# Spline weight stages: small tables spread inside SBUF instead of full-height tables, and DMAs moved between three queues

## The chip, the cores and the metric

The kernel runs on the 8 cores of one Trainium2 chip, each core with its own quarter-batch half and no exchange between cores. The time is the device time of the slowest core, in microseconds.

## The reference

One transformer layer in "sandwich" form over x of shape (4, 2048, 2048): attention (16 heads, causal), then a gated feed-forward network whose three weight matrices are not given but are interpolated from control points.

```python
def spline_reconstruct(control_points, out_size, in_size):
    n = out_size * in_size
    idx, f = _catmull_rom_grid(control_points.shape[0], n)   # n_ctrl = n / 128.9
    p0, p1, p2, p3 = (control_points[idx[k]] for k in range(4))
    w = 0.5*(2*p1 + (p2-p0)*f + (2*p0-5*p1+4*p2-p3)*f**2 + (3*p1-p0-3*p2+p3)*f**3)
    return w.reshape(out_size, in_size)

gate_w, up_w = spline_reconstruct(gate_cp, 8192, 2048), spline_reconstruct(up_cp, 8192, 2048)
down_w = spline_reconstruct(down_cp, 2048, 8192)

x = x + layernorm(attention(layernorm(x)))
h = layernorm(x)
x = x + layernorm((silu(h @ gate_w.T) * (h @ up_w.T)) @ down_w.T)
```

## The kernel before

Each core builds all three weight matrices for itself and holds them in DRAM (`wbuf_g`, `wbuf_u`, `wbuf_d`). 128 consecutive weights form a block that spans at most two spline segments, so a block's weights are a product of 16 numbers (4 control points times 4 powers of a position) with a fixed 16x128 matrix (`atsb`), once for each of the two segments; a byte mask says for each weight which of the two holds. There are NBLK = 131072 blocks.

**Gate/up stage** (`make_gu_gen`, the first stage, 64 chunks of GCH = 2048 blocks). Per chunk:

1. `ldtoks(c)` loads two fp32 tables of 128 rows, `cpr0` (control points) and `tpr0` (powers), on GpSimd's queue, cast to bf16 in flight, into `gi0`, `gi1` (2 buffers each). Many of the 128 rows are repeats: only 10 rows of control points and 8 of powers are distinct.
2. `umult(c)` (VectorE, L363) multiplies them into `Ug`.
3. For the gate tile (w = 0), then for the up tile (w = 1), four groups of 512 blocks: two matmuls (L396) into `pguA`, `pguB`; ScalarE copies `pguB` to `gwo` (L412); VectorE overwrites it from `pguA` where the mask `gm` is set (L417). These last are called evictions here.
4. After four groups SyncE's queue stores the tile: `wbuf_g`, then `wbuf_u`, 512 KB each. `gwo` has two buffers, one for each w, so ScalarE's first copy of a tile waits for that tile's store in the chunk before. Behind the up store SyncE's queue loads the mask for chunk c+2.

The loads for c+1 are written ahead of the matmuls of c and wait for `umult(c-1)`.

**Down stage** (`make_down_gen`, 32 chunks of DCH = 4096 blocks, after attention and the output projection). The same with one tile of eight groups a chunk, tables of 64 rows (`cpr1`, `tpr1`), and lines L465 (multiply), L495 (matmuls), L509 (copy), L513 (eviction). Its store is 1 MB in runs of 64 bf16 numbers (128 B), 8192 of them, into `wbuf_d`; `dwo` has two buffers, by c % 2. Store and mask load (`dm`, 512 KB) share SyncE's queue.

Engines run their instructions in program order. A DMA stands in the order of its issuing engine, and whatever it waits for holds what is behind it. `Sched` writes the order out by hand: letters T, V, S, G, Y are TensorE, VectorE, ScalarE, GpSimd, SyncE. All DMA issues show line L160.

The stages between and after (`x2T` norm and transpose, QKV projection `pq` L629, attention, output projection `po` L843, feed-forward `pgE` L1021, `puE` L1027, `pdE` L1070) are separated from these two by barriers on all engines.

Of the kernel before, what the change touches and what calls it, by code (L numbers as in the profile page):

```python
# [10 lines left out]
F32 = mybir.dt.float32  # L11
BF16 = mybir.dt.bfloat16
# [3 lines left out]
AP = bass.AP  # L16

B, S, D = 4, 2048, 2048
# [4 lines left out]
NBLK = NSAMP // 128  # L23
GCH = 2048
NGCH = NBLK // GCH
DCH = 4096
NDCH = NBLK // DCH
# [252 lines left out]
def build_program():  # L280
    nc = bass.Bass("TRN2", target_bir_lowering=False)
    sch = Sched()
# [5 lines left out]
    bout_d = nc.dram_tensor("bout_rep", [128, D], F32, kind="ExternalInput")  # L288
    cpr0 = nc.dram_tensor("cpr0", [128, NBLK], F32, kind="ExternalInput")
    cpr1 = nc.dram_tensor("cpr1", [64, NBLK], F32, kind="ExternalInput")  # L290
    tpr0 = nc.dram_tensor("tpr0", [128, NBLK], F32, kind="ExternalInput")
    tpr1 = nc.dram_tensor("tpr1", [64, NBLK], F32, kind="ExternalInput")
# [17 lines left out]
    with ctx:  # L310
# [20 lines left out]

        def make_gu_gen(wc, pA, pB, depth):
            U = [wc.enter_context(nc.sbuf_tensor(f"Ug{i}", [128, GCH], BF16))
                 for i in range(2)]
# [5 lines left out]
                nc.sbuf_tensor(f"gm_{i}", [128, GCH], mybir.dt.uint8))  # L340
                for i in range(2)]
            WO = [wc.enter_context(nc.sbuf_tensor(f"gwo_{i}", [128, GCH], BF16))
                  for i in range(2)]
            streams = [(wbuf_g, 0, 32), (wbuf_u, 64, 96)]

            def ldtoks(c):
                t0 = sch.dma("G", IN0[c % 2][:, :],
                             AP(cpr0, c * GCH, [[NBLK, 128], [1, GCH]]),
                             f"wg{c % 2}")
                t1 = sch.dma("G", IN1[c % 2][:, :],  # L350
                             AP(tpr0, c * GCH, [[NBLK, 128], [1, GCH]]),
                             f"wg{c % 2}")
                return (t0, t1)

            def gen():
                umark, evmark, stok, mtoks, ltok = {}, {}, {}, {}, {}

                def umult(c):
                    sch.wait("V", ltok[c][0])
                    sch.wait("V", ltok[c][1])  # L360
                    if c >= 2:
                        sch.wait("V", evmark[(c - 2) * 8 + 7])
                    sch.op("V", lambda v, b=c % 2: v.tensor_mul(  # L363
                        U[b][:, :], IN0[b][:, :], IN1[b][:, :]))
                    umark[c] = sch.mark("V")

                for c in range(NGCH):
                    yield
                    buf = c % 2
                    if c == 0:  # L370
                        for cpre in (0, 1):
                            mtoks[cpre] = sch.dma(
                                "Y", MSK[cpre % 2][:, :],
                                wgm_gu_d[:, cpre * GCH:(cpre + 1) * GCH],
                                f"gm{cpre % 2}")
                        ltok[0] = ldtoks(0)
                        umult(0)
                    if c + 1 < NGCH:
                        if c >= 1:
                            sch.wait("G", umark[c - 1])  # L380
                        ltok[c + 1] = ldtoks(c + 1)
                    sch.wait("T", umark[c])
                    for w in range(2):
# [3 lines left out]
                        for q4 in range(4):  # L387
# [21 lines left out]
                            wo_ap = WO[cw % 2][:, q4 * 512:(q4 + 1) * 512]  # L409
                            mk_ap = MSK[c % 2][:, q4 * 512:(q4 + 1) * 512]  # L410
                            sch.op("S", lambda s, o_=wo_ap, pp=pB[bk]:
# [6 lines left out]
                            evmark[i2] = sch.mark("V")  # L418
                        sch.wait("Y", evmark[c * 8 + w * 4 + 3])
                        stok[cw] = sch.dma(  # L420
                            "Y", wb[:, c * GCH:(c + 1) * GCH],
                            WO[cw % 2][:, :],
                            f"ws{cw % 2}")
                    if c + 2 < NGCH:
                        sch.wait("Y", evmark[c * 8 + 7])
                        mtoks[c + 2] = sch.dma(
                            "Y", MSK[c % 2][:, :],
                            wgm_gu_d[:, (c + 2) * GCH:(c + 3) * GCH],
                            f"gm{c % 2}")
                    if c + 1 < NGCH:  # L430
# [4 lines left out]

        def make_down_gen(wc, pA, pB, depth):
            Ud = [wc.enter_context(nc.sbuf_tensor(f"Ud{i}", [64, DCH], BF16))
                  for i in range(2)]
# [5 lines left out]
                nc.sbuf_tensor(f"dm_{i}", [128, DCH], mybir.dt.uint8))  # L444
                for i in range(2)]
            WO = [wc.enter_context(nc.sbuf_tensor(f"dwo_{i}", [128, DCH], BF16))
                  for i in range(2)]
            NCG = DCH // 512

            def ldtoks(c):  # L450
                sch.dma("G", IN0[c % 2][:, :],
                        AP(cpr1, c * DCH, [[NBLK, 64], [1, DCH]]),
                        f"wd{c % 2}")
                return sch.dma("G", IN1[c % 2][:, :],
                               AP(tpr1, c * DCH, [[NBLK, 64], [1, DCH]]),
                               f"wd{c % 2}")

            def gen():
                umark, evmark, stok, mtoks, ltok = {}, {}, {}, {}, {}

                def umult(c):
                    sch.wait("V", ltok[c])
                    if c >= 2:
                        sch.wait("V", evmark[(c - 2) * NCG + NCG - 1])
                    sch.op("V", lambda v, b=c % 2: v.tensor_mul(  # L465
                        Ud[b][:, :], IN0[b][:, :], IN1[b][:, :]))
                    umark[c] = sch.mark("V")

                for c in range(NDCH):
                    yield  # L470
                    buf = c % 2
                    if c == 0:
                        for cpre in (0, 1):
                            mtoks[cpre] = sch.dma(
                                "Y", MSK[cpre % 2][:, :],
                                wgm_dn_d[:, cpre * DCH:(cpre + 1) * DCH],
                                f"dm{cpre % 2}")
                        ltok[0] = ldtoks(0)
                        umult(0)
                    if c + 1 < NDCH:  # L480
                        if c >= 1:
                            sch.wait("G", umark[c - 1])
                        ltok[c + 1] = ldtoks(c + 1)
                    sch.wait("T", umark[c])
                    first_ev = True
                    for cg in range(NCG):
# [14 lines left out]
                        if first_ev:  # L501
                            if c >= 2:
# [3 lines left out]
                        wo_ap = WO[buf][:, cg * 512:(cg + 1) * 512]  # L506
                        mk_ap = MSK[c % 2][:, cg * 512:(cg + 1) * 512]
                        sch.op("S", lambda s, o_=wo_ap, pp=pB[bk]:
# [14 lines left out]
                    if c + 2 < NDCH:  # L523
                        mtoks[c + 2] = sch.dma(
                            "Y", MSK[c % 2][:, :],
                            wgm_dn_d[:, (c + 2) * DCH:(c + 3) * DCH],
                            f"dm{c % 2}")
                    if c + 1 < NDCH:
# [616 lines left out]
def _perm_gu():  # L1145
    if "gu" not in _TPR:
        p = np.arange(GCH).reshape(GCH // 16, 16).T.ravel()
        _TPR["gu"] = (np.arange(NBLK).reshape(-1, GCH)[:, p]).ravel()
    return _TPR["gu"]


def _perm_dn():
    if "dn" not in _TPR:
        p = np.arange(DCH).reshape(DCH // 64, 64).T.ravel()
        _TPR["dn"] = (np.arange(NBLK).reshape(-1, DCH)[:, p]).ravel()
    return _TPR["dn"]


def _tpr0():
    if 0 not in _TPR:  # L1160
        cst = _consts()
        _TPR[0] = np.ascontiguousarray(
            cst["taupow"][cst["r0_tau"]][:, _perm_gu()])
    return _TPR[0]


def _tpr1():
    if 1 not in _TPR:
        cst = _consts()
        _TPR[1] = np.ascontiguousarray(  # L1170
            cst["taupow"][cst["r1_tau"]][:, _perm_dn()])
    return _TPR[1]
# [57 lines left out]
```

How the kernel before makes its waits and increments, by code:

```python
            def f(eng):  # L196
                for fn, waits, incs, _isdma in self.recs[e]:
                    agg = {}
                    for (sn, v) in waits:
                        agg[sn] = max(agg.get(sn, 0), v)
                    for sn, v in agg.items():
                        eng.wait_ge(sems[sn], v)
                    inst = fn(eng)
                    for (sn, n, _tgt) in incs:
                        inst.then_inc(sems[sn], n)
```

## Time and profile before

| | us |
|---|---|
| median of 2 runs | 4481.23 (4478.77 to 4483.7) |
| the profiled execution | 4469.14 |
| its span, slowest core (core 4) | 4467.6 |
| spans of the other cores | 4446.7 to 4462.4 |
| granted TensorE clock, mean | 0.869 to 0.871 |

The profile is of one execution on its slowest core. Busy time counts instructions of an engine; DMA share is the mean busy share of 16 DMA engines. SPq, ACTq and POOLq are the queues in which SyncE, ScalarE and GpSimd issue DMAs.

### The profile page before, as it was taken

Reading aid. Unit: us, or ns where it says so; the run is one execution under the profiler, and the core shown is the slowest. Engines: PE = TensorE matmul, PEld = TensorE weight load, DVE = VectorE, ACT = ScalarE, POOL = GpSimd, SP = SyncE. Lnnn points to the kernel's source line nnn. Section 1 sums busy time; section 2 is a strip of 40 time slices with the busy share of each in tenths; the row PEclk is TensorE's granted clock in tenths of the full one; section 3 lists DMA queues with packets and bytes.
Section 4 is the critical chain, followed back from the end, with each engine's and each line's share of the span. In section 5 each row is a group of like instructions: output and inputs, shape, how many; then the busy total and the mean of one; then the engine's idle time right before and its main releaser. Section 6 shows DMA issues by size and latency. Waiting matters only on the chain.

```text
span 4467.6 us, 40618 instructions; the slowest of 8 cores (4446.7 to 4467.6 us)
## 1 busy us (share of the span) xinstructions
PE 2937.2 (66%) x12618; PEld 1171.4 (26%) x12832; DVE 1419.7 (32%) x1868; ACT 924.6 (21%) x1519; POOL 139.9 (3%) x232
## 2 busy tenths in 40 slices
PE   2333333299999567676922222289998947999895
PEld 0000111244444111111410000044443323444332
DVE  4555565722222343433064544411000032001002
ACT  3344443200000334333112322200000021000001
POOL 1000000000000000000000000000000000000000
PEclk9999999999999777777955555589999978999997
DMA  9999997364443100000549999944433444444344
GB/s 173 191 206 206 211 211 193 122 79 74 76 76 67 58 19 29 29 29 11 84 157 162 160 157 158 147 151 152 155 145 111 138 149 158 151 151 152 108 137 141
DMA packets 588577, 567.97 MB, mean 127 GB/s; under 512 B 280016, under 2 KB 495056, under 8 KB 576976
## 3 DMA queue, kind: packets, MB, share of 16 engines
q1 hardware_dynamic: 498640, 431.11, 35.9%
q0 software_dynamic: 89728, 134.25, 20.4%
q8 instruction: 110, 1.80, 0.2%
q14 instruction: 99, 0.81, 0.1%
HBM read 565.31 MB, written 134.22 MB: 157 GB/s over the span
## 4 chain that ended last, share of the span: by engine, by line
PE 49%; DMA 25%; DVE 15%; SPq 4%; issue 4%; ACT 3%; DVEq 0%; ACTq 0%; another core or an unknown queue 0%; POOL 0%; POOLq 0%
PE pq L629 12%; DMA wbuf_g<-gwo 10%; PE puE L1027 10%; PE pgE L1021 10%; PE pdE L1070 6%; DMA wdsb<-wbuf_d 5%; DMA dm<-wgmask_dn 5%; SPq L160 4%; DVE gwo L417 4%; PE prow L222 3%; PE pav L226 3%; PE psc L764 3%; PE po L843 2%; DVE rs L799 2%; DVE colsb L236 2%
## 5 line engine op out<-in xcount | busy, mean ns | idle before, releaser
L1027 PE MATMUL puE<-x2f,wusb 128*128 128x512 bf16 x2048 | 778.4, 380 | 22.7 <-DMA wusb<-wbuf_u 18.5
L1021 PE MATMUL pgE<-x2f,wgsb 128*128 128x512 bf16 x1966 | 747.0, 380 | 0.0
L396 PE MATMUL pguA<-Ug,atsb 16*128 16x512 bf16 x512 | 267.4, 597 | 479.7 <-DVE Ug L363 266.3
L629 PE MATMUL pq<-x2T,wq 128*128 128x512 bf16 x2508 | 551.6, 380 | 17.8 <-DMA wq<-wqkvT 15.1
L1070 PE MATMUL pdE<-actsb,wdsb 128*128 128x512 bf16 x2006 | 458.4, 382 | 54.1 <-DMA wdsb<-wbuf_d 51.0
L417 DVE CAST_PREDICATED gwo<-gm,pguA 128x512 bf16<-128x512 uint8 x512 | 353.7, 691 | 301.6 <-ACT gwo L412 254.8
L495 PE MATMUL pdnA<-Ud,atsb 16*128 16x512 bf16 x256 | 133.7, 597 | 407.9 <-DVE dwo L513 214.4
L412 ACT CAST gwo<-pguB 128x512 bf16<-128x512 f32 x512 | 299.6, 585 | 435.5 <-DMA wbuf_g<-gwo 378.5
L1042 DVE TENSOR_TENSOR actsb<-silsb,puE 128x512 bf16<-128x512 bf16 x128 | 88.1, 688 | 819.0 <-ACT silsb L1037 819.0
L629 PEld LDWEIGHTS pq<-x2T,wq 128*128 128x128 bf16 x2560 | 250.9, 98 | 318.3 <-issue 17.6
L775 ACT ACTIVATE pT<-psc 128x512 bf16<-128x512 f32 x384 | 229.3, 597 | 330.5 <-PE psc L764 289.8
L1070 PEld LDWEIGHTS pdE<-actsb,wdsb 128*128 128x128 bf16 x2048 | 195.2, 98 | 317.3 <-issue 103.8
L396 PE MATMUL pguB<-Ug,atsb 16*128 16x512 bf16 x512 | 274.8, 613 | 0.0
L1021 PEld LDWEIGHTS pgE<-x2f,wgsb 128*128 128x128 bf16 x2048 | 200.9, 98 | 261.0 <-issue 20.8
L1027 PEld LDWEIGHTS puE<-x2f,wusb 128*128 128x128 bf16 x2048 | 200.8, 98 | 242.7 <-issue 2.4
L513 DVE CAST_PREDICATED dwo<-dm,pdnA 128x512 bf16<-128x512 uint8 x256 | 176.9, 691 | 258.8 <-DMA dm<-wgmask_dn 214.4
L1037 ACT ACTIVATE silsb<-pgE 128x512 bf16<-128x512 f32 x128 | 76.4, 597 | 792.3 <-PE puE L1027 792.2
L396 PEld LDWEIGHTS pguA<-Ug,atsb 16*128 16x128 bf16 x512 | 56.5, 110 | 683.8 <-issue 683.7
L509 ACT CAST dwo<-pdnB 128x512 bf16<-128x512 f32 x256 | 149.8, 585 | 384.2 <-DMA wbuf_d<-dwo 189.1
L764 PE MATMUL psc<-qall,kb 128*128 128x512 bf16 x375 | 172.1, 473 | 76.7 <-DVE attnout L713 54.5
L649 DVE TENSOR_SCALAR kst<-pq,bqkvsb 128x512 bf16<-128x512 f32 x128 | 96.1, 751 | 346.0 <-PE pq L629 346.0
L782 DVE TENSOR_TENSOR pT<-pT,cmasksb 128x512 bf16<-128x512 bf16 x256 | 109.0, 426 | 299.7 <-ACT pT L775 298.0
(76 smaller groups left out, 1960.5 us busy)
## 6 DMA issues: line engine op xcount, KB each, us to landing
wgsb<-wbuf_g SPq DMA_DIRECT2D x128, 512.0 KB, 3.7
wusb<-wbuf_u SPq DMA_DIRECT2D x128, 512.0 KB, 4.6
wdsb<-wbuf_d SPq DMA_DIRECT2D x128, 512.0 KB, 3.7
gi<-cpr POOLq DMA_DIRECT2D x64, 512.0 KB, 9.4
gi<-tpr POOLq DMA_DIRECT2D x64, 512.0 KB, 12.4
wbuf_g<-gwo SPq DMA_DIRECT2D x64, 512.0 KB, 7.3
wbuf_u<-gwo SPq DMA_DIRECT2D x64, 512.0 KB, 5.1
wbuf_d<-dwo SPq DMA_DIRECT2D x32, 1024.0 KB, 18.5
```

The costliest lines, as they stand in the source:

```text
L160: [lambda eng, o=out, i=in_: eng.dma_start(out=o, in_=i), w, [(sname, 16, tgt)], True])
L396: t.matmul(pp[:, :], at_sb[u_:u_ + 16, :], U[b][u_:u_ + 16, cc:cc + 512], start=True, stop=True, tile_position=(u_, 0)))
L412: s.copy(o_, pp[:, :]))
L417: v.copy_predicated(o_, m_, pp[:, :]))
L509: s.copy(o_, pp[:, :]))
L513: v.copy_predicated(o_, m_, pp[:, :]))
L629: t.matmul(pq[bi][:, :], wq[(o // 2) % 2][:, h * 256 + (o % 2) * 128: h * 256 + (o % 2) * 128 + 128], x2T[:, h * S + g * 512:h * S + g * 5 ...
L764: t.matmul(psc[c % 4][:, :], kb[b][:, c * 128:c * 128 + 128], q_all[:, hh * TPC + ts * 512: hh * TPC + ts * 512 + 512], start=True, stop=T ...
L775: s.activation(pT[b][:, c * 512:c * 512 + 512], psc[c % 4][:, :], AF.Exp, bias=0.0, scale=SCALE))
L1021: t.matmul(pg[bi][:, :], wg[o % 4][:, h * 128:h * 128 + 128], x2f[:, h * 512:h * 512 + 512], start=(h == 0), stop=(h == 15)))
L1027: t.matmul(pu[bi][:, :], wu[o % 4][:, h * 128:h * 128 + 128], x2f[:, h * 512:h * 512 + 512], start=(h == 0), stop=(h == 15)))
L1070: t.matmul(pd[bi + o][:, :], wd[(i_ // 8) % 2][:, (i_ % 8) * 256 + o * 128: (i_ % 8) * 256 + o * 128 + 128], act[:, i_ * 512:i_ * 512 + 51 ...
```

## The change

The change touches only the two weight stages.

- The tables are loaded small: for gate/up 10 rows of control points (`tap_gu`) and 32 of powers (`tau_gu`: 8 distinct rows, repeated to 32) into a new tile `gct`; for down 5 and 32 rows into `dct`. Still on GpSimd's queue, still cast.
- A new function `expand(c)` copies them inside SBUF into the 128-row (64-row) tiles by DMAs on ScalarE's queue, eight of 16 rows x 4 KB a chunk in gate/up, four of 16 rows x 8 KB in down. Rows that hold nothing are zeroed once by VectorE. `expand(c+1)` stands in ScalarE's program order after the gate tile of chunk c (gate/up) or after the fifth of eight groups (down), and waits for the loads of c+1.
- `umult(c)` waits for the spreads. The loads for c+1 wait for the spreads of c-1 and not for `umult(c-1)`.
- Mask loads move from SyncE's to ScalarE's queue, three chunks ahead instead of two, with four buffers instead of two.
- Stores alternate: gate tiles and even down chunks on SyncE's queue, up tiles and odd down chunks on GpSimd's.

The diff, cut to its core (down follows gate/up; its differing lines are shown):

```diff
@@ make_gu_gen
             def ldtoks(c):
-                t0 = sch.dma("G", IN0[c % 2][:, :],
-                             AP(cpr0, c * GCH, [[NBLK, 128], [1, GCH]]),
-                             f"wg{c % 2}")
-                t1 = sch.dma("G", IN1[c % 2][:, :],
-                             AP(tpr0, c * GCH, [[NBLK, 128], [1, GCH]]),
-                             f"wg{c % 2}")
-                return (t0, t1)
+                sch.dma("G", CT[c % 2][0:10, :],
+                        AP(tap_gu_d, c * GCH, [[NBLK, 10], [1, GCH]]),
+                        f"wg{c % 2}")
+                return sch.dma("G", CT[c % 2][10:42, :],
+                               AP(tau_gu_d, c * GCH, [[NBLK, 32], [1, GCH]]),
+                               f"wg{c % 2}")
...
+                def expand(c):
+                    sch.wait("S", ltok[c])
+                    if c >= 2:
+                        sch.wait("S", umark[c - 2])
+                    else:
+                        sch.wait("S", msmk_gu)
+                    for si in range(4):
+                        wt, dlt = si // 2, si % 2
+                        sch.dma("S", AP(IN0[c % 2], (si * 32) * GCH,
+                                        [[GCH, 16], [1, GCH]]),
+                                AP(CT[c % 2], (wt * 5 + dlt) * GCH,
+                                   [[GCH, 4], [0, 4], [1, GCH]]),
+                                f"we{c % 2}")
+                        etok[c] = sch.dma(
+                            "S", AP(IN1[c % 2], (si * 32) * GCH,
+                                    [[GCH, 16], [1, GCH]]),
+                            AP(CT[c % 2], (10 + dlt * 16) * GCH,
+                               [[GCH, 16], [1, GCH]]),
+                            f"we{c % 2}")
...
                 def umult(c):
-                    sch.wait("V", ltok[c][0])
-                    sch.wait("V", ltok[c][1])
+                    sch.wait("V", etok[c])
...
                     if c + 1 < NGCH:
                         if c >= 1:
-                            sch.wait("G", umark[c - 1])
+                            sch.wait("G", etok[c - 1])
                         ltok[c + 1] = ldtoks(c + 1)
...
-                        sch.wait("Y", evmark[c * 8 + w * 4 + 3])
+                        stq = "Y" if cw % 2 == 0 else "G"
+                        sch.wait(stq, evmark[c * 8 + w * 4 + 3])
                         stok[cw] = sch.dma(
-                            "Y", wb[:, c * GCH:(c + 1) * GCH],
+                            stq, wb[:, c * GCH:(c + 1) * GCH],
                             WO[cw % 2][:, :],
                             f"ws{cw % 2}")
-                    if c + 2 < NGCH:
-                        sch.wait("Y", evmark[c * 8 + 7])
-                        mtoks[c + 2] = sch.dma(
-                            "Y", MSK[c % 2][:, :],
+                        if w == 0 and c + 1 < NGCH:
+                            expand(c + 1)
+                    if c + 3 < NGCH:
+                        if c >= 1:
+                            sch.wait("S", evmark[(c - 1) * 8 + 7])
+                        mtoks[c + 3] = sch.dma(
+                            "S", MSK[(c + 3) % 4][:, :],
...
@@ make_down_gen
+                    for si in range(2):
+                        sch.dma("S", AP(IN0[c % 2], (si * 32) * DCH,
+                                        [[DCH, 16], [1, DCH]]),
+                                AP(CT[c % 2], si * DCH,
+                                   [[DCH, 4], [0, 4], [1, DCH]]),
+                                f"de{c % 2}")
...
+                        if cg == NCG // 2 and c + 1 < NDCH:
+                            expand(c + 1)
                     od = DCH // 64
-                    sch.wait("Y", evmark[c * NCG + NCG - 1])
+                    stq = "Y" if c % 2 == 0 else "G"
+                    sch.wait(stq, evmark[c * NCG + NCG - 1])
                     stok[c] = sch.dma(
-                        "Y",
+                        stq,
                         AP(wbuf_d, c * od,
                            [[64 * D, 128], [D, 64], [1, od]]),
                         AP(WO[buf], 0, [[DCH, 128], [od, 64], [1, od]]),
...
```

## Rows read from the trace of the kernel before

**Rows 1.** The page: span, and the chain that ended last by line.

```profile
span 4467.6 us, 40618 instructions; the slowest of 8 cores (4446.7 to 4467.6 us)
...
PE pq L629 12%; DMA wbuf_g<-gwo 10%; PE puE L1027 10%; PE pgE L1021 10%; PE pdE L1070 6%; DMA wdsb<-wbuf_d 5%; DMA dm<-wgmask_dn 5%; SPq L160 4%; DVE gwo L417 4%; PE prow L222 3%; PE pav L226 3%; PE psc L764 3%; PE po L843 2%; DVE rs L799 2%; DVE colsb L236 2%
```

**Rows 2.** Busy us by stage, engine by engine; then clock, DMA share, GB/s.

```profile
13.00:762.00 749.00, 276.70 (x1024) 72.16 (x1024) 432.19 (x576) 300.86 (x513) 65.44 (x124) 1.00 0.95 201
...
2341.00:2880.00 539.00, 138.38 (x512) 36.02 (x512) 249.94 (x288) 149.78 (x256) 33.19 (x64) 0.50 1.21 156
```

**Rows 3.** Timeline of gate/up chunks: start, us, engine, line, instruction, idle before.

```profile
423.99 0.32 SPq L160 DMA_DIRECT2D wbuf_u<-gwo  x1
424.02 1.23 DVE L363 TENSOR_TENSOR Ug<-gi 128x2048 bf16<-128x2048 bf16 x1
...
425.40 0.60 PE L396 MATMUL pguB<-Ug,atsb 16*128 16x512 bf16 x1
...
427.89 4.62 ACT L412 CAST gwo<-pguB 128x512 bf16<-128x512 f32 x7 [5.66 <-DMA wbuf_g<-gwo]
...
431.79 0.32 SPq L160 DMA_DIRECT2D wbuf_g<-gwo  x1
```

**Rows 4.** Gate stores by tensor: issue ns, first and last start.

```profile
L160 SPq DMA_DIRECT2D wbuf_g<-gwo x64: 319/320/326, 26.0 to 755.7; - x64
```

**Rows 5.** DMA queues in 100 us of the gate/up stage: packets, MB, share.

```profile
DMA packets 6448, 21.16 MB, mean 212 GB/s; under 512 B 714, under 2 KB 714, under 8 KB 6442
...
q0 software_dynamic: 2554, 9.31, 57.5%
q1 hardware_dynamic: 3888, 11.80, 37.9%
```

**Rows 6.** Down stores by tensor: issue ns, first and last start.

```profile
L160 SPq DMA_DIRECT2D wbuf_d<-dwo x32: 524/525/2850, 2365.3 to 2866.8; - x32
```

**Rows 7.** SyncE's queue in the down stage, first chunks.

```profile
2365.32 0.61 SPq L160 DMA_DIRECT2D wbuf_d<-dwo  x1
2365.98 7.83 SPq L160 DMA_DIRECT2D dm<-wgmask_dn  x1
```

**Rows 8.** Timeline of down chunks, later: SyncE's queue and VectorE.

```profile
2592.96 2.28 DVE L465 TENSOR_TENSOR Ud<-di 64x4096 bf16<-64x4096 bf16 x1
2593.49 15.42 SPq L160 DMA_DIRECT2D dm<-wgmask_dn  x1
...
2596.95 6.25 DVE L513 CAST_PREDICATED dwo<-dm,pdnA 128x512 bf16<-128x512 uint8 x8 [1.71 <-ACT dwo L509]
```

**Rows 9.** DMA queues in 440 us of the down stage.

```profile
q1 hardware_dynamic: 222455, 41.58, 83.1%
```

**Rows 10.** Chain in order of time: the last down store.

```profile
2866.82 12.84 DMA wbuf_d<-dwo
```

**Rows 11.** GpSimd's DMA issues by tile: count | busy, mean ns.

```profile
L160 POOL DMA_DIRECT2D gi<-cpr x64 | 33.9, 530 | 656.4 <-DVE Ug L363 653.8 <-POOLq L177 2.6
L160 POOL DMA_DIRECT2D wq<-wqkvT x24 | 27.4, 1143 | 641.8 <-PE pq L629 486.8 <-DVE x2T L583 155.0
```

**Rows 12.** DMA queues in 110 us of the QKV projection.

```profile
q0 software_dynamic: 15342, 7.79, 54.5%
```

**Rows 13.** DMA queues in 200 us of the down projection.

```profile
q1 hardware_dynamic: 53766, 27.11, 46.1%
```

**Rows 14.** GB/s in 40 slices of 23 us, K and V loads alone.

```profile
GB/s 0 12 130 313 233 235 317 354 383 385 385 351 356 392 385 413 413 399 427 385 427 363 178 57 0 0 0 0 0 0 0 0 0 0 0 0 0 0 0 0
```

**Rows 15.** A SyncE issue behind two others: ns.

```profile
L160 SPq DMA_DIRECT2D bqkvsb<-bqkv x1: 432/432/432, 2.0 to 2.0; - x1
```

**Rows 16.** DMA issues, whole run: count, KB each, median us to landing.

```profile
wgsb<-wbuf_g SPq DMA_DIRECT2D x128, 512.0 KB, 3.7
...
kvbuf<-kst SPq DMA_DIRECT2D x128, 128.0 KB, 1.8
...
atsb<-atilde POOLq DMA_DIRECT2D x4, 4.0 KB, 2.3
```

More of the change, by code:

```diff
@@ L332, in make_gu_gen @@
         def make_gu_gen(wc, pA, pB, depth):
+            CT = [wc.enter_context(nc.sbuf_tensor(f"gct{i}", [42, GCH], BF16))
+                  for i in range(2)]
             U = [wc.enter_context(nc.sbuf_tensor(f"Ug{i}", [128, GCH], BF16))
@@ L340, in make_gu_gen @@
                 nc.sbuf_tensor(f"gm_{i}", [128, GCH], mybir.dt.uint8))
-                for i in range(2)]
+                for i in range(4)]
             WO = [wc.enter_context(nc.sbuf_tensor(f"gwo_{i}", [128, GCH], BF16))
@@ L436, in make_down_gen @@
         def make_down_gen(wc, pA, pB, depth):
+            CT = [wc.enter_context(nc.sbuf_tensor(f"dct{i}", [37, DCH], BF16))
+                  for i in range(2)]
             Ud = [wc.enter_context(nc.sbuf_tensor(f"Ud{i}", [64, DCH], BF16))
@@ L444, in make_down_gen @@
                 nc.sbuf_tensor(f"dm_{i}", [128, DCH], mybir.dt.uint8))
-                for i in range(2)]
+                for i in range(4)]
             WO = [wc.enter_context(nc.sbuf_tensor(f"dwo_{i}", [128, DCH], BF16))
@@ L448, in make_down_gen, with expand @@
             NCG = DCH // 512
+            for t in IN0 + IN1:
+                sch.op("V", lambda v, t_=t: v.memset(t_[:, :], 0.0))
+            msmk_dn = sch.mark("V")
             def ldtoks(c):
-                sch.dma("G", IN0[c % 2][:, :],
-                        AP(cpr1, c * DCH, [[NBLK, 64], [1, DCH]]),
+                sch.dma("G", CT[c % 2][0:5, :],
+                        AP(tap_dn_d, c * DCH, [[NBLK, 5], [1, DCH]]),
                         f"wd{c % 2}")
-                return sch.dma("G", IN1[c % 2][:, :],
-                               AP(tpr1, c * DCH, [[NBLK, 64], [1, DCH]]),
+                return sch.dma("G", CT[c % 2][5:37, :],
+                               AP(tau_dn_d, c * DCH, [[NBLK, 32], [1, DCH]]),
                                f"wd{c % 2}")
             def gen():
-                umark, evmark, stok, mtoks, ltok = {}, {}, {}, {}, {}
+                umark, evmark, stok, mtoks = {}, {}, {}, {}
+                ltok, etok = {}, {}
+                def expand(c):
+                    sch.wait("S", ltok[c])
+                    if c >= 2:
+                        sch.wait("S", umark[c - 2])
+                    else:
+                        sch.wait("S", msmk_dn)
+                    for si in range(2):
[4 more added lines that the diff above has]
+                                f"de{c % 2}")
+                        etok[c] = sch.dma(
+                            "S", AP(IN1[c % 2], (si * 32) * DCH,
+                                    [[DCH, 16], [1, DCH]]),
+                            AP(CT[c % 2], (5 + si * 16) * DCH,
+                               [[DCH, 16], [1, DCH]]),
+                            f"de{c % 2}")
                 def umult(c):
-                    sch.wait("V", ltok[c])
+                    sch.wait("V", etok[c])
                     if c >= 2:
@@ L481, in gen @@
                         if c >= 1:
-                            sch.wait("G", umark[c - 1])
+                            sch.wait("G", etok[c - 1])
                         ltok[c + 1] = ldtoks(c + 1)
@@ L522, in gen @@
                         f"dws{c % 2}")
[L523 to L527, printed above, removed]
+                    if c + 3 < NDCH:
+                        if c >= 1:
+                            sch.wait("S", evmark[(c - 1) * NCG + NCG - 1])
+                        mtoks[c + 3] = sch.dma(
+                            "S", MSK[(c + 3) % 4][:, :],
+                            wgm_dn_d[:, (c + 3) * DCH:(c + 4) * DCH],
+                            f"dm{(c + 3) % 4}")
                     if c + 1 < NDCH:
@@ L1156, in _perm_dn, with _tau_tiled @@
     return _TPR["dn"]
+def _tau_tiled():
+    cst = _consts()
+    tp = cst["taupow"]
+    return np.concatenate([np.tile(tp[0:4], (4, 1)), np.tile(tp[4:8], (4, 1))])
 def _tpr0():
     if 0 not in _TPR:
-        cst = _consts()
-        _TPR[0] = np.ascontiguousarray(
-            cst["taupow"][cst["r0_tau"]][:, _perm_gu()])
+        _TPR[0] = np.ascontiguousarray(_tau_tiled()[:, _perm_gu()])
     return _TPR[0]
@@ L1168, in _tpr1 @@
     if 1 not in _TPR:
[L1169 to L1171 removed]
+        _TPR[1] = np.ascontiguousarray(_tau_tiled()[:, _perm_dn()])
     return _TPR[1]
@@ L1197 @@
     taps = [c[cst["tapidx"]] for c in cps]
-    cpr0 = np.ascontiguousarray(
-        np.stack([taps[cst["r0_wt"][p]][cst["r0_tap"][p]]
-                  for p in range(128)])[:, _perm_gu()])
-    cpr1 = np.ascontiguousarray(
-        np.stack([taps[2][cst["r1_tap"][p]]
-                  for p in range(64)])[:, _perm_dn()])
+    tap_gu = np.ascontiguousarray(
+        np.concatenate([taps[0], taps[1]])[:, _perm_gu()])
+    tap_dn = np.ascontiguousarray(taps[2][:, _perm_dn()])
     wgm_gu = np.ascontiguousarray(cst["wgmask"][:, _perm_gu()])
```

40 lines of the change are left out of this document (23 added, 17 removed).

## The prediction

> **What bounds the kernel now.** I read the page first (span 4467.6 us, and which lines the end hangs on), then the busy time by stage. The chain names the store of the gate weights with 10%, the mask load of the down weights with 5%, and SyncE's own queue with 4% [rows 1]. These belong to the two stages that the change touches: gate/up (749 us, DMA engines 0.95 busy) and down (539 us, share 1.21, which is over 1 because packets of two queues overlap) [rows 2]. Everything else I take as unchanged.
>
> The gate/up stage runs 64 chunks. Gate stores start from 26.0 to 755.7 us, so a chunk is 729.7/63 = 11.58 us [rows 4]. The reader sees in the timeline that from the first of four copies of a tile to its store is 431.79 - 427.89 = 3.9 us, and that ScalarE stood idle 5.66 us ahead of that copy until the last gate store had landed [rows 3]. Without that wait the first copy could start when the matmul ends, 425.40 + 0.60 = 426.0, that is 2.0 us after the up store's issue. So 427.9 - 426.0 = 1.9 us of each chunk is that wait (a chunk without it: 2.0 + 3.9 + 3.2 = 9.1). Under it lies the traffic: 21.16 MB written in 100 us, and the 9.31 MB of the casting queue are read as twice that, 30.5 MB in 95 busy us, so 320 GB/s [rows 5]. A chunk reads or writes 2.10 MB of fp32 tables, 0.26 of mask and 1.05 of stores, 3.41 MB: 10.7 us of the 11.58.
>
> The down stage runs 32 chunks: 501.5/31 = 16.2 us each, 32.4 a pair [rows 6]. SyncE's queue never rests: the store with its 8192 runs of 128 B issues in 0.5 us, and the mask load behind it is held 15.42 us [rows 8]. A run costs 0.831 x 440 x 16/222455 = 26.3 ns of a DMA engine [rows 9].
>
> **Gate/up, step by step.** Traffic per chunk falls to 0.34 (42 rows of 8 KB) + 0.26 + 1.05 + 0.52 of spreads = 2.18 MB, 6.8 us at 320 GB/s. That is cover won, but the order of the queues decides. I count from the end of chunk c-1 (its last eviction), time 0.
>
> GpSimd's queue then has, in this order, the up store of c-1 and the two loads for c+1; the wait ahead of the loads is over by then. Issues are 0.53 us each [rows 11]. Ahead of the last byte are 0.52 + 0.34 MB on that queue and the mask's 0.26: 1.13 MB, 3.5 us. Start 0.3, and 2.3 us of fixed cost, which a 4 KB load on this queue shows [rows 16]: the loads land at 6.1.
>
> ScalarE: multiply 1.23 us and matmul, first copy at 2.0, last copy of the gate tile at about 5.1 (5.9 less the last eviction). It now waits for the loads until 6.1, with the four up copies queued behind the waiting DMA. VectorE's evictions, the up store and the next loads wait for those. Then it issues 8 spreads. The trace shows no DMA issue on ScalarE; the bounds are SyncE's 0.32 us [rows 3] and its 0.43 behind others [rows 15], and as eight follow one another I take 0.42: 3.4 us. Then 3.9 us for the up tile. Chunk: 6.1 + 3.4 + 3.9 = 13.4 us, 1.8 more than before, x64 = +115. With loads early enough (by 5.1) and 0.32 it is 9.0 + 8 x 0.32 = 11.6: nothing. With loads 1.4 later than mine and 0.43 it is 14.8: +206. Below nothing only if an issue costs under 0.32. The spreads must land 3.9 us after the last issue to cost nothing: a 128 KB transfer took 1.8 [rows 16]. The mask issue on ScalarE lies under the 2.0 us of multiply and matmul, the memsets under the first load. The gate store's wait is gone: it has 7 us since its issue.
>
> **Down, step by step.** Time 0 is the end of an odd chunk c-1, whose store goes to GpSimd's queue, with the loads for c+1 behind it. Issue: 1.14 us for 2048 runs against 0.53 for 128 [rows 11], so about 3 us for 8192, which draining overlaps. The drain is the great unknown: no row has 128 B runs on this queue. Bounds: 20.6 ns a run, from the last store, 12.84 us with 512 runs an engine and 2.3 fixed [rows 10], and 62.5 ns, this queue's cost of a run of 1016 B read (0.545 x 110 x 16/15342) [rows 12]. Between them: bytes alone go at 400 GB/s [rows 14], 25 an engine, so 41 ns of the 62.5 are bytes and 22 are the run. SyncE's 504 B runs cost 0.461 x 200 x 16/53766 = 27.4 [rows 13], 20 of it bytes, 7 the run. This queue costs 14.7 more a run; on 26.3 that gives 41.0, x512 = 21.0 us. The loads land at 1.0 + 21.0 + 1.9 (0.61 MB) + 2.3 = 26.2. I call this x.
>
> ScalarE is at its spread for c+1 after 2.3 + 1.7 + 3.2 = 7.2 us (multiply, matmul and start, five copies) [rows 8]. It stands till x; 4 issues make 1.7, three more groups 3.0: chunk c ends at x+4.7. The spreads (0.5 MB) are in at x+5, after 1.7 of issues and the 3.3 or so that rows of such size suggest (3.7 for 512 KB [rows 16]). Then 7.2 us to the spread for c+2: x+12.2. Its loads are there. But chunk c's store went out on SyncE's queue at x+4.7, and if ScalarE's queue shares what holds SyncE's, the hold is 0.61 + 7.83 = 8.4 us for a store on an idle queue [rows 7], until x+13.1. Then 1.7 + 3.0: the pair takes x+17.8 = 44.0 us, 11.6 over 32.4, x16 = +186. Without any hold 0.9 less a pair (14 in all); at 20.6 ns a run +18.
>
> Sum: the profiled execution took 4469, 12 under the median of 4481. I add to the median: 4481 + 115 + 186 = 4782.
>
> **Rivals.**
> - Slow drain: the whole 62.5 ns a run hold here too. 11.0 us more a pair, +176: 4958. For it: same queue. Against: 41 ns of that are bytes.
> - Long hold: a ScalarE issue behind SyncE's store is held 15.9 us as in later chunks [rows 8]. To x+20.6 instead of x+13.1: +120: 4902. Against: those 15.4 hold the backlog of the store before, and there is half as much now. The Trainium skill (DMA: Bandwidth & Descriptors, Queues, rings and completion order) says that SyncE and ScalarE own rings but no descriptor generator of their own, which speaks for this hold; the rows have no second hardware queue to show it.
> - Slow spreads: the tap spreads read few partitions, and if each goes at one engine's 25 GB/s (as above), four of 64 KB take 10.5 us, landed 12.3 after the first issue. Gate/up then turns on 12.3 + 5.1 = 17.4 us, 4.0 x 64 = +256; down +6.4 a pair, +102: 5140. Nothing in the rows speaks for or against. The Trainium skill (same page, Why a DMA increments its semaphore by 16 and not by 1) gives a DMA the largest engine count that divides both slowest dimensions; by it these have four engines, not one, and would be in time.
> - Faster: the loads pass the store in front of them and land by 7.2 us. Then ScalarE waits nowhere for them: gate/up 11.6 with issues of 0.32, down 7.2 + 16.9 = 24.1 a pair, -8.3 x 16 = -133: 4348. It gains 2% from x under 9.9. Against: before, the second load of a pair lands after the first, as in one line.
> - No change: loads by 5.1 and issues of 0.32 in gate/up (+0), 20.6 ns a run in down (x = 15.7, pair 33.5, +18): 4499.
>
> **How the numbers follow.** Forecast 0.42, slow drain 0.12, long hold 0.12, slow spreads 0.08, faster 0.10, no change 0.16. The forecast's own range, from its bounds: 4600 to 4930. The range over all leaves out faster and slow spreads (0.18) and takes in the others: 4450 to 5000. Over 2% (90 us, about what a measurement tells) faster: 0.10. Within: 0.16 and 0.02 of the forecast's low end, 0.18. Slower: 0.72.
>
> **What would show it.** Gate stores 13.4 us apart; ScalarE idle about 1 us before its spreads for the loads, and 0.4 us an issue; no wait of ScalarE for the gate store. In down: pairs of 44 us, ScalarE waiting some 19 us a pair for the loads; GpSimd's store 23 us or so to landing. Wrong if ScalarE issues in 0.1 us, if down loads land before the store ahead of them, or if another stage moves.

## The result, and the profile after

| | before | after |
|---|---|---|
| median, us | 4482.8 | 5221.4 |
| ratio | 1 | 1.165 (1.163 to 1.167) |
| span of the profiled execution | 4467.6 | 5211.5 |

The change makes the kernel 16.5% slower, 739 us. The prediction said 4782, in a range of 4450 to 5000: the sign was right, the size was not, and the time lies outside the range.

The page of the kernel after, its span, DMA share in 40 slices, and the chain that ended last by line:

```profile
span 5211.5 us, 41718 instructions; the slowest of 8 cores (5182.5 to 5211.5 us)
...
DMA  3444444444454431000054666665444344444344
...
ACTq L160 15%; PE pq L689 10%; PE pgE L1081 9%; PE puE L1087 9%; PE pdE L1130 5%; DMA wdsb<-wbuf_d 4%; DMA gct<-tau_gu 4%; DMA dct<-tau_dn 4%; DVE gwo L442 4%; DMA di<-dct 3%; PE pav L226 2%; PE prow L222 2%; PE psc L824 2%; PE po L903 2%; DVE rs L859 2%
```

The queue in which ScalarE issues its DMAs (ACTq) leads the chain with 15%, and the DMA engines are busy 3 or 4 tenths in the first stage, where their share was 0.95 before [rows 2]: the traffic fell as planned, and the time rose. By stage, the windows of after (columns as in [rows 2]: window, busy us of PE, PEld, DVE, ACT, POOL, clock, DMA share, GB/s):

```profile
13.00:1268.00 1255.00, 276.42 (x1024) 72.05 (x1024) 433.91 (x577) 300.85 (x513) 97.45 (x188) 1.00 0.40 102
1268.00:2840.00 1572.00, 1164.05 (x4896) 443.77 (x4896) 548.01 (x736) 322.21 (x522) 36.58 (x32) 0.86 0.30 67
2840.00:3620.00 780.00, 138.22 (x512) 35.87 (x512) 263.81 (x292) 149.78 (x256) 76.13 (x80) 0.50 0.64 99
3620.00:5211.00 1591.00, 1378.36 (x6400) 619.78 (x6400) 189.14 (x264) 151.76 (x228) 0.00 (x0) 0.94 0.43 143
```

Gate/up takes 1255 us where it took 749 [rows 2], down 780 where it took 539. Between them 1572 us stand against 1579 before, and after them 1591 against 1587. So the loss lies in the two stages, 506 + 241 us. Gate stores and down stores by tensor (issue ns min/median/max, first and last start), after:

```profile
L160 SPq DMA_DIRECT2D wbuf_g<-gwo x64: 319/320/326, 34.0 to 1260.0; - x64
...
L160 SPq DMA_DIRECT2D wbuf_d<-dwo x16: 512/513/612, 2887.1 to 3592.9; - x16
```

A gate/up chunk takes (1260.0 - 34.0)/63 = 19.46 us where it took 11.58 [rows 4], 7.88 x 64 = +504. A pair of down chunks takes (3592.9 - 2887.1)/15 = 47.05 where it took 32.4 [rows 6], 14.7 x 16 = +234. One chunk of gate/up after, the timeline, to be read beside [rows 3]:

```profile
514.43 1.23 DVE L387 TENSOR_TENSOR Ug<-gi 128x2048 bf16<-128x2048 bf16 x1
514.89 0.55 POOL L160 DMA_DIRECT2D wbuf_u<-gwo  x1 [18.02 <-DVE gwo L442]
...
515.93 0.51 POOL L160 DMA_DIRECT2D gct<-tau_gu  x1
...
516.62 2.60 ACT L437 CAST gwo<-pguB 128x512 bf16<-128x512 f32 x4 [3.51 <-PE pguB L421]
...
519.82 9.86 ACTq L160 DMA_DIRECT2D gi<-gct  x8
520.51 0.32 SPq L160 DMA_DIRECT2D wbuf_g<-gwo  x1
...
529.88 2.60 ACT L437 CAST gwo<-pguB 128x512 bf16<-128x512 f32 x4 [10.67 <-issue]
530.64 3.07 DVE L442 CAST_PREDICATED gwo<-gm,pguA 128x512 bf16<-128x512 uint8 x4 [10.20 <-ACT gwo L437]
...
533.81 1.23 DVE L387 TENSOR_TENSOR Ug<-gi 128x2048 bf16<-128x2048 bf16 x1
534.27 0.56 POOL L160 DMA_DIRECT2D wbuf_u<-gwo  x1 [17.84 <-DVE gwo L442]
```

The multiply starts at 514.43, when the up tile of the chunk before is done. GpSimd issues the up store and both loads in 1.6 us. ScalarE makes its four gate copies from 516.62 and is at its spreads by 519.2; at 519.82 the loads are in. So far 5.4 us. Then ScalarE issues eight spreads, 9.86 us, in which no copy is made; VectorE stands idle for 10.20. From 529.88 come four copies, and the chunk ends at 533.7. Of 19.3 us, half is the issuing. Over the whole stage the average chunk is 5.6 us to the first issue, 9.7 for the eight issues and 4.2 to the next multiply.

### The profile page after: what moved, and what is told of

Its sections match the earlier page's. It is cut to its first block, busy times and chain, and to the rows that moved or that the text cites. A ratio compares the mean times of both kernels' runs of the same rounds, so it can differ in the third digit from the quotient of the medians.

```text
span 5211.5 us, 41718 instructions; the slowest of 8 cores (5182.5 to 5211.5 us)
## 1 busy us (share of the span) xinstructions
PE 2957.1 (57%) x12832; PEld 1171.5 (22%) x12832; DVE 1440.4 (28%) x1876; ACT 924.6 (18%) x1519; POOL 214.5 (4%) x312
## 3 DMA queue, kind: packets, MB, share of 16 engines
q0 software_dynamic: 87424, 104.63, 11.8%
## 4 chain that ended last, share of the span: by engine, by line
PE 43%; DMA 18%; ACTq 15%; DVE 13%; issue 4%; ACT 3%; POOL 2%; DVEq 0%; SPq 0%; POOLq 0%
ACTq L160 15%; PE pq L689 10%; PE pgE L1081 9%; PE puE L1087 9%; PE pdE L1130 5%; DMA wdsb<-wbuf_d 4%; DMA gct<-tau_gu 4%; DMA dct<-tau_dn 4%; DVE gwo L442 4%; DMA di<-dct 3%; PE pav L226 2%; PE prow L222 2%; PE psc L824 2%; PE po L903 2%; DVE rs L859 2%
## 5 line engine op out<-in xcount | busy, mean ns | idle before, releaser
L1081 PE MATMUL pgE<-x2f,wgsb 128*128 128x512 bf16 x2048 | 779.1, 380 | 12.3 <-DMA wusb<-wbuf_u 12.3
L550 PEld LDWEIGHTS pdnA<-Ud,atsb 16*128 16x128 bf16 x256 | 28.1, 110 | 749.6 <-issue 749.6
```

Source lines behind the costliest of these rows:

```text
L550: t.matmul(pp[:, :], at_sb[u_:u_ + 16, :], Ud[b][u_:u_ + 16, cc:cc + 512], start=True, stop=True, tile_position=(u_, 0)))
L1081: t.matmul(pg[bi][:, :], wg[o % 4][:, h * 128:h * 128 + 128], x2f[:, h * 512:h * 512 + 512], start=(h == 0), stop=(h == 15)))
```

## Experiments

Ratios are against the kernel before on the same chip; its median there was 4483 to 4540 us.

**Which rows a spread reads.** Two kernels leave the number of spreads, their bytes and destinations and change only what the tap spreads read. In both the weights computed are not the reference's.

```diff
@@ e1_sixteen_rows (down alike)
                                 AP(CT[c % 2], (wt * 5 + dlt) * GCH,
-                                   [[GCH, 4], [0, 4], [1, GCH]]),
+                                   [[GCH, 16], [1, GCH]]),
@@ e2_four_rows_apart (down alike)
-                                   [[GCH, 4], [0, 4], [1, GCH]]),
+                                   [[4 * GCH, 4], [0, 4], [1, GCH]]),
```

> The changed kernel, but each of the tap spreads (gate/up and down) reads 16 neighbouring rows of the small tile instead of 4 rows four times each. The number of DMAs, their bytes and their destinations stay; the weights computed are not the reference's. Theory 'few source rows': ScalarE is held 9.87 us by eight spreads of a gate/up chunk because 64 KB come out of four neighbouring rows; with 16 rows an issue takes 0.54 us (the shortest in the trace), 4.3 us for eight, a chunk 13.9 instead of 19.46 us: -355 us in gate/up, and in down four issues in 2.2 instead of 6.5 and spreads landed about as early, 12 us less a pair of 47, -190: about 4680. Rival 'issues': ScalarE's queue takes only a few DMAs at a time, whatever they read: the hold stays over 8 us and the time over 5050.

> The changed kernel, but the four rows that a tap spread reads (still four times each) are four partitions apart instead of neighbours; the weights computed are not the reference's. Theory 'neighbouring partitions share a way out': in the trace the packets of a tap spread take about 640 ns when four run at once and 159 ns alone, so four rows far apart go at four times the rate and this run is as fast as the one with 16 rows. Rival 'four DMA engines': a spread whose source has four rows runs on four engines, wherever the rows lie; then it is between, with the hold closer to 9.87 than to 4.3. Rival 'issues': no change, 5221.

Measured: 4847 us (1.071 of the kernel before, 1.057 to 1.084) with sixteen rows; 4869 (1.075, 1.062 to 1.089) with four rows apart. The eight issues of one gate/up chunk (ns min/median/max, start of the first and of the last), in the kernel after, with sixteen rows, and with four rows apart:

```profile
L160 ACTq DMA_DIRECT2D gi<-gct x8: 536/1040/2651, 519.8 to 529.1; - x8
```

```profile
L160 ACTq DMA_DIRECT2D gi<-gct x8: 537/612/618, 535.6 to 540.0; - x8
```

```profile
L160 ACTq DMA_DIRECT2D gi<-gct x8: 536/686/756, 540.3 to 545.2; - x8
```

From the first start to the end of the last: 9.86 us after, 5.0 with sixteen rows, about 5.4 with four rows apart. In these chunks the longest issue falls from 2.65 us to 0.62 and 0.76. The chunk shown with sixteen rows is among the quickest of its run, so here are all 512 issues of the stage, in the same order:

```profile
L160 ACTq DMA_DIRECT2D gi<-gct x512: 536/727/3057, 15.0 to 1249.3; - x171
```

```profile
L160 ACTq DMA_DIRECT2D gi<-gct x512: 514/611/2042, 15.0 to 1017.2; - x171
```

```profile
L160 ACTq DMA_DIRECT2D gi<-gct x512: 536/710/1742, 15.3 to 1023.9; - x171
```

On average eight issues take 9.7 us after, 5.9 with sixteen rows and 5.7 with four rows apart; single issues of up to 2.0 and 1.7 us remain. Four rows read four times each go as fast as sixteen rows, provided they are four partitions apart. So neither the number of distinct rows nor the repeated reading makes the difference of 4 us; it is that the four rows are neighbours. The rival 'four DMA engines' falls: the source has four rows here too. The rival 'issues' falls with it, in part: even with sixteen rows an issue takes 0.51 us at least and 0.61 as the median, and not 0.32 as on SyncE for 128 rows [rows 3].

The longest issue of the chunk after, 2.65 us, is close to 64 KB at the 25 GB/s of one engine, 2.6 us, which the prediction's slow-spread rival had worked out. The packets of the first tap spread (rows 0 to 3), counted in the trace, say more: after, four packets of 4 KB are under way at a time, and the fifth to eighth of a chunk take 640 ns each (median), so 4 x 4096 / 640 = 26 GB/s in all; with the rows four partitions apart the same packets take 240 ns, the first four 160. The Trainium skill (SBUF — State Buffer, Door 1: The DMA port swizzle) puts partitions 0 to 3 on one of 16 ports, with 27.6 GB/s measured; an estimate by it is 2.4 us for 64 KB out of these four, and rows 0, 4, 8 and 12 lie on four ports. These two runs agree, with 26 GB/s from the packets and 2.65 us of hold. By that section of the Trainium skill the other three tap spreads (rows 1 to 4, 5 to 8, 6 to 9) straddle two ports; no run here prices them one by one. The rule that the prediction cited (the Trainium skill, DMA: Bandwidth & Descriptors, Why a DMA increments its semaphore by 16 and not by 1) gives such a spread four engines; four packets at a time agree with it, and it does not help while all four take their data from neighbouring rows.

Gate stores with sixteen rows, gate stores with four rows apart, by tensor:

```profile
L160 SPq DMA_DIRECT2D wbuf_g<-gwo x64: 319/320/326, 29.6 to 1028.1; - x64
```

```profile
L160 SPq DMA_DIRECT2D wbuf_g<-gwo x64: 319/319/327, 30.6 to 1034.6; - x64
```

A chunk is 15.85 and 15.94 us. Expected were 13.9: the first issue came 5.8 us (sixteen rows) and 6.1 us (four apart) after the multiply's start and not 5.4, and the eight took 5.9 and 5.7 and not 4.3. In down a pair falls to 37.9 with sixteen rows, 9.2 less where 12 were expected, and to 38.9 with four rows apart. ScalarE's waits for the loads behind GpSimd's store do not shrink there (232 us in 16 waits with sixteen rows, 210 in 15 after). So the time missed the 4680 expected in both stages. The down stores with sixteen rows:

```profile
L160 SPq DMA_DIRECT2D wbuf_d<-dwo x16: 512/513/607, 2653.9 to 3222.0; - x16
```

**The same spreads on SyncE's queue** (gate/up only).

```diff
                 def expand(c):
-                    sch.wait("S", ltok[c])
+                    sch.wait("Y", ltok[c])
...
-                        sch.dma("S", AP(IN0[c % 2], (si * 32) * GCH,
+                        sch.dma("Y", AP(IN0[c % 2], (si * 32) * GCH,
```

> The changed kernel, but the gate/up spreads are issued on SyncE's queue, behind the gate store, instead of ScalarE's; down as changed. Theory: the hold falls on whatever engine issues. ScalarE's 9.87 us are gone from the path between the gate and the up tile, but spreads start only after the gate store and take some 11 us to land, then 5.9 us to the next gate store: 16.9 us a chunk instead of 19.5, -165 us, 5055. If the hold were a matter of ScalarE's queue alone, SyncE would issue eight in 3.5 us, and a chunk would take 10 to 11 us: about 4650.

Measured: 5253 us (1.160, 1.146 to 1.174), no better than the changed kernel's 1.165. The timeline of one chunk with the spreads on SyncE's queue:

```profile
533.51 0.32 SPq L160 DMA_DIRECT2D wbuf_g<-gwo  x1
...
533.99 10.39 SPq L160 DMA_DIRECT2D gi<-gct  x8
...
547.23 1.23 DVE L387 TENSOR_TENSOR Ug<-gi 128x2048 bf16<-128x2048 bf16 x1 [10.63 <-DMA gi<-gct]
...
553.33 0.33 SPq L160 DMA_DIRECT2D wbuf_g<-gwo  x1
```

SyncE is held 10.39 us by the same eight issues: the hold belongs to the transfers, not to ScalarE. I had expected 16.9 us a chunk, and it is 553.33 - 533.51 = 19.8. The term at fault is the landing: the multiply starts 13.2 us after the first issue, not 11. ScalarE is free now, but spreads start behind the gate store and end 13 us later, so the chain runs through them instead of through ScalarE.

**Is an issue on ScalarE held by SyncE's store of 8192 runs?** The kernel before, with only its mask loads moved (down is shown, gate/up alike).

```diff
                     if c + 2 < NDCH:
+                        sch.wait("S", evmark[c * NCG + NCG - 1])
                         mtoks[c + 2] = sch.dma(
-                            "Y", MSK[c % 2][:, :],
+                            "S", MSK[c % 2][:, :],
```

> The kernel before, with nothing changed but the mask loads of both stages, issued by ScalarE instead of SyncE, at the same point (after a chunk's last eviction). It asks whether an issue on ScalarE is held by the 8192-run store that SyncE issued just before. If the two share what holds SyncE's next issue: ScalarE held 8 to 15 us a chunk in down, its next copies late by as much, down no faster than the 16.2 us a chunk of before: 4450 to 4600. If not: an issue of 0.35 us, the mask lands early, and down is bounded by the store alone, 12.8 to 15 us a chunk: 40 to 110 us faster, 4370 to 4440. Gate/up unchanged in both.

Measured: 4562 us (1.006 of the kernel before, 1.000 to 1.011). Its mask loads and its down stores by tensor:

```profile
L160 ACTq DMA_DIRECT2D dm<-wgmask_dn x32: 334/334/453, 2395.2 to 2929.9; - x32
```

```profile
L160 SPq DMA_DIRECT2D wbuf_d<-dwo x32: 512/560/17388, 2419.4 to 2956.7; - x32
```

All 32 mask issues, 30 of them at the moment when SyncE's store goes out, took 0.33 to 0.45 us; SyncE's own store behind a store was held up to 17.4 us. ScalarE is not held by SyncE's transfers. It is held by its own: in the kernel after, where the same mask loads follow four spreads in ScalarE's queue, their median issue takes 2.9 us, and with sixteen rows or four rows apart 0.33 us again. The mask issues after:

```profile
L160 ACTq DMA_DIRECT2D dm<-wgmask_dn x32: 343/2891/3082, 2839.7 to 3544.5; - x32
```

The prediction's 8.4 us of hold and its rival of 15.9 were both wrong, and so was my reading of the Trainium skill (DMA: Bandwidth & Descriptors, Queues, rings and completion order), that queues without a descriptor generator of their own must hold one another: in this run the one did not hold the other. The hoped-for gain did not come either. A down chunk takes (2956.7 - 2419.4)/31 = 17.3 us: without a mask load between them the stores of SyncE's queue still hold one another. Gate/up, expected unchanged, takes 12.45 us a chunk in this trace where it took 11.58. These two can't be laid on the moved masks alone: the kernel before was itself 58 us slower on this chip (4540), and against it the run is level.

**The place of the loads behind the store** (down alike; both stages load their first two chunks ahead).

```diff
-                    if c + 1 < NGCH:
-                        if c >= 1:
-                            sch.wait("G", etok[c - 1])
-                        ltok[c + 1] = ldtoks(c + 1)
+                    if c + 2 < NGCH:
+                        sch.wait("G", etok[c])
+                        ltok[c + 2] = ldtoks(c + 2)
```

> The changed kernel, but the small tables of chunk c+2 are loaded as soon as the spreads of chunk c have landed, ahead of chunk c's store in GpSimd's queue, in both stages. It asks what the place of the loads behind the store costs. Down: the loads land 16.5 us after the odd store now, and ScalarE would be at its spread after 7.2 us; so the pair falls from 47.1 to about 38 us, -145 us. Gate/up: ScalarE would be there after 5.1 us and the loads land after 5.4, so the wait was nearly hidden and a chunk stays at 19 us (-0.3 x 64 = -20). Together about 5055. Rival: the down pair is bound by the drain of 2 x 8192 runs and the loads only hide it: then it stays over 44 us, over 5120.

Measured: 5081 us (1.130, 1.125 to 1.134). Gate and down stores by tensor, loads ahead:

```profile
L160 SPq DMA_DIRECT2D wbuf_g<-gwo x64: 319/320/330, 33.7 to 1201.1; - x64
```

```profile
L160 SPq DMA_DIRECT2D wbuf_d<-dwo x16: 512/513/612, 2828.1 to 3453.5; - x16
```

A gate/up chunk is 18.53 us (0.9 less, 60 us), a down pair 41.7 (5.4 less, 86 us). Expected were 19 and 38. Every multiply of the down stage waits for its spreads to land, 167 us in 32 waits (132 after), so loads that come early only lengthen that wait. Those issued behind GpSimd's store land later, 16 us after the first issue against 13; that the draining store slows them is likely and not shown.

**Both edits at once.**

> The changed kernel with both edits at once: the tap spreads read 16 neighbouring rows (so the weights computed are not the reference's), and the small tables are loaded two chunks ahead, in front of the store. What is left against the version with half tables is then only that ScalarE issues spreads between its copies. If the parts add up, a gate/up chunk is 5.1 us to the last gate copy + 5.2 for eight issues + 3.9 to the up store + 0.3 = 14.5 us, against 9.6 with half tables and 15.85 with sixteen rows alone; a down pair is 2 x (10.3 + 3.4) = 27.4 us plus what the stores' drain holds, so 28 to 32: together 4530 to 4620, level with or up to 3% slower than the kernel before. Rival: the eight issues hide once the loads are early, and gate/up is under 12 us, faster than before.

Its edit is the sum of the two diffs above. Measured: 4725 us in the profiled execution, with the kernel before at 4509 on the same chip, so about 1.05, with no interval; expected were 4530 to 4620. One chunk, and the stores by tensor:

```profile
526.63 0.56 POOL L160 DMA_DIRECT2D wbuf_u<-gwo  x1 [13.22 <-DVE gwo L442]
...
530.49 6.48 ACTq L160 DMA_DIRECT2D gi<-gct  x8
...
537.93 3.07 DVE L442 CAST_PREDICATED gwo<-gm,pguA 128x512 bf16<-128x512 uint8 x4 [5.76 <-ACT gwo L437]
```

```profile
L160 SPq DMA_DIRECT2D wbuf_g<-gwo x64: 319/320/327, 30.0 to 959.2; - x64
...
L160 SPq DMA_DIRECT2D wbuf_d<-dwo x16: 512/513/612, 2588.3 to 3111.1; - x16
```

A gate/up chunk is 14.75 us, as expected (14.5). With rows and loads mended, ScalarE still issues between its copies, for 6.48 us here and 6.2 on average (5.2 expected), and that keeps the stage above the 11.58 of before. The pair, 34.85, missed its 28 to 32. In the trace its two rows of four issues differ, 3.5 us on average after SyncE's store and 6.6 after GpSimd's (3.4 expected for both), and the multiply waits for the landing both times. Why GpSimd's store goes with the long ones stays open.

**Without any spread.** The tables of before, of which only the rows in use are loaded, now two chunks ahead; in down stores in two queues, and masks on ScalarE's queue with four buffers.

```diff
             def ldtoks(c):
-                t0 = sch.dma("G", IN0[c % 2][:, :],
-                             AP(cpr0, c * GCH, [[NBLK, 128], [1, GCH]]), ...
+                for si in range(4):
+                    sch.dma("G", IN0[c % 2][si * 32:si * 32 + 16, :],
+                            AP(cpr0, si * 32 * NBLK + c * GCH,
+                               [[NBLK, 16], [1, GCH]]), f"wg{c % 2}")
+                    t = sch.dma("G", IN1[c % 2][si * 32:si * 32 + 16, :], ...
...
-                        ltok[c + 1] = ldtoks(c + 1)
+                        sch.wait("G", umark[c])
+                        ltok[c + 2] = ldtoks(c + 2)
```

> A version of the kernel before, without any spread: only the 16 of each 32 table rows that the matmuls read are loaded, straight from DRAM in pieces of 16 rows (eight a chunk in gate/up, four in down), two chunks ahead and in front of the store; gate/up stores and masks as in the kernel before; in down odd chunks are stored on GpSimd's queue and the masks are loaded on ScalarE's with four buffers. If the gate/up stage of before is bound by its 3.41 MB a chunk, 2.36 MB (7.4 us at 320 GB/s) put it close to the 9.1 us that copies and evictions need: 9.1 to 10, -100 to -155 us. In down two queues store in turn: 12 to 14 us a chunk instead of 16.2, -70 to -135 us. Together 4190 to 4310. Rival: pieces of 16 rows go as slowly as four rows did, and loads come late: gate/up at 12 us or more, no gain over the kernel before.

Measured: 4331 us, 0.963 of the kernel before (0.960 to 0.966), faster than both. One chunk of gate/up, from up store to up store, and the stores by tensor:

```profile
410.81 0.32 SPq L160 DMA_DIRECT2D wbuf_u<-gwo  x1
...
413.03 5.31 ACT L417 CAST gwo<-pguB 128x512 bf16<-128x512 f32 x8 [3.98 <-PE pguB L401]
...
413.78 6.25 DVE L422 CAST_PREDICATED gwo<-gm,pguA 128x512 bf16<-128x512 uint8 x8 [1.71 <-ACT gwo L417]
...
420.10 0.32 SPq L160 DMA_DIRECT2D wbuf_u<-gwo  x1
```

```profile
L160 SPq DMA_DIRECT2D wbuf_g<-gwo x64: 319/319/326, 30.2 to 634.5; - x64
...
L160 SPq DMA_DIRECT2D wbuf_d<-dwo x16: 512/513/612, 2260.3 to 2711.0; - x16
```

ScalarE copies eight groups in a row and waits for no DMA; a chunk is (634.5 - 30.2)/63 = 9.59 us, against 9.1 from copies and evictions alone. In the whole stage ScalarE waits for a gate store 8 times, 42 us in all, where it did so 60 times before, 379 us. This fits a stage of before bound by its 3.41 MB, of which 2.36 are left; but the loads also come a chunk earlier, and no run takes the two apart. A down pair is (2711.0 - 2260.3)/15 = 30.0 us, 2.4 less than before, where 24 to 28 were expected: ScalarE still waits for stores to land, 224 us in 17 waits. So the time lies 21 us above the 4190 to 4310 expected.

## Why the prediction was right or wrong

**What held.** The other stages did not move. The wait of ScalarE for the gate store went, and the DMA share fell (0.95 to 0.40 in gate/up). The order of the queues decided, as said: the gate/up chunk is the path through ScalarE, 5.4 us to the first issue in the chunk shown (6.1 predicted), the issues, and 4.0 to the last eviction (3.9 predicted).

**The term that failed: eight issues, 3.4 us predicted, 9.7 measured.** I priced an issue from SyncE's issues of 128 rows, 0.32 to 0.43, and took these as both bounds. But none of those rows was of a transfer that drains slowly. A row of such a one had been read: SyncE's mask load is held 15.42 us behind a slow store [rows 8]. I used that only for stores. Each tap spread drains slowly, and an issue behind it is held on the engine that issues. This term alone is 6.3 us of an average chunk, 405 us. The forecast is 439 us short: 389 in gate/up, where the first issue came 0.5 us earlier than priced on average and the part behind the issues took 0.3 more, and 48 in down. The issues of down are mis-sized likewise, 1.7 against 6.5 a chunk.

**The rival that came closest** was the slow spreads, at 5140. Its 25 GB/s for four neighbouring rows agrees with the packets of rows 0 to 3, and its landing, 12.3 us after the first issue, with the last spread packet of a chunk, 11.8 on average. It was wrong in where the cost falls: it left the issues at 3.4 us, so ScalarE made its up copies while the spreads landed (17.4 us a chunk). In fact ScalarE stands still in the issues, and the landing hides behind the copies that follow. I gave it 0.08 on the ground that nothing in the rows spoke for it, and the range left it out; its bound should have been in the range as that of an unknown cost. Even so 5140 would have been 81 us short. The forecast's own range of 4600 to 4930 is narrower than its bounds: they add up to 4499 (the case of no change) and 4481 + 206 + 362 = 5049, and the measured time lies outside these too.

**Down was nearly right in sum, by luck: two errors cancelled.** A pair of 44.0 was predicted and 47.05 came. One pair after, from odd store to odd store:

```profile
3236.41 2.76 POOL L160 DMA_DIRECT2D wbuf_d<-dwo  x1 [41.81 <-DVE dwo L568]
...
3252.94 6.37 ACTq L160 DMA_DIRECT2D di<-dct  x4
...
3260.21 2.28 DVE L568 CAST_PREDICATED dwo<-dm,pdnA 128x512 bf16<-128x512 uint8 x3 [12.47 <-ACT dwo L564]
...
3267.18 2.28 DVE L519 TENSOR_TENSOR Ud<-di 64x4096 bf16<-64x4096 bf16 x1 [4.69 <-DMA di<-dct]
...
3271.18 3.87 DVE L568 CAST_PREDICATED dwo<-dm,pdnA 128x512 bf16<-128x512 uint8 x5 [1.71 <-ACT dwo L564]
...
3273.24 6.49 ACTq L160 DMA_DIRECT2D di<-dct  x4
...
3283.71 2.75 POOL L160 DMA_DIRECT2D wbuf_d<-dwo  x1 [42.54 <-DVE dwo L568]
```

The loads are in at 3252.94, 16.5 us after the odd store, where I had 26.2. The drain of small runs on GpSimd's queue was priced at 41 ns a run; issues and landings of after show what it is:

```profile
wbuf_d<-dwo SPq DMA_DIRECT2D x16, 1024.0 KB, 11.3
wbuf_d<-dwo POOLq DMA_DIRECT2D x16, 1024.0 KB, 12.6
...
gct<-tau_gu POOLq DMA_DIRECT2D x64, 128.0 KB, 3.8
...
dct<-tau_dn POOLq DMA_DIRECT2D x32, 256.0 KB, 13.5
```

12.6 us to landing on GpSimd's queue and 11.3 on SyncE's: (12.6 - 2.3)/512 = 20 ns a run, the low bound [rows 10]. My 14.7 ns more a run on this queue, drawn from a casting load of 1016 B, do not carry over to a store of 128 B. On the other side, from that point to the end of the pair it took 30.8 us and not 17.8. The multiply (3267.18) waits for the spreads until 14.2 us after the first issue instead of 5; the first 6.4 us of issues lie within this. From there to the next issues are 6.1 (7.2 predicted), and these take 6.5 where I had 1.7 and the rest 4.0 where I had 3.0. The hold by SyncE's store, 0.9 us of the forecast, is nothing (the run with moved masks).

**Where the 7.88 us of a gate/up chunk come from**, in the order in which the runs take them off: 19.46 as changed; 3.6 for neighbouring source rows (15.85 with sixteen); 1.1 for the loads behind the store (14.75 with both); 5.2 for what remains of spreads on ScalarE (9.59 without, in a kernel that also loads its tables otherwise, so this last step is not of a single cause). Read this way, the change removes what bound the stage before, worth 11.58 - 9.59 = 2.0 us, and pays 9.9 for it.

## What to carry to other kernels

A DMA costs its issuing engine little only while its queue drains; here eight small copies held theirs for 5.7 us at best, and for 9.7 where they drained slowly. So do not put a row of DMAs between the copies that the next store waits for. Moving them to an idle engine frees this one, but gains nothing where their landing is then on the path (1.160 against 1.165). Count what a DMA reads as well as what it writes: 64 KB out of partitions 0 to 3 went at about one engine's rate, though they filled sixteen rows. Fewer bytes from DRAM are worth having if the transfers that replace them are not on the path; here a kernel that loads half the rows, two chunks ahead, with down's stores in two queues, was 3.7% faster, and loading a sixth and copying the rest inside SBUF lost 16.5%.

## What the runs showed of the hardware

- Eight issues of 64 KB copies inside SBUF, four of them out of four neighbouring partitions: 9.7 us on average, the longest issue 3.06; the same with the rows four partitions apart: 5.7 and 1.74; with sixteen rows: 5.9 and 2.04.
- 4 KB packets out of partitions 0 to 3, four at a time: about 640 ns each; the same packets with the rows four partitions apart: 240.
- An issue of a 16-row spread takes at least 0.51 us on ScalarE and 0.53 on SyncE, more than the 0.32 of a 128-row store.
- ScalarE's mask issues (0.33 us) are not held while SyncE's queue holds SyncE for up to 17.4 us; behind ScalarE's own slow spreads they take 2.9 (median).
- 8192 runs of 128 B stored from GpSimd's queue land in 12.6 us, from SyncE's in 11.3, when they alternate; GpSimd's issue takes 2.76 us.
